# Splitting a unit's five blocks 4 + 1 instead of 3 + 2 over two transposing banks of an attention block

## The chip, the core and the metric

The kernel runs on one core of a Trainium2 chip. The metric is the device time of one execution in microseconds (us). Of the core's engines five matter here: TensorE (PE in the profile, its weight loads PEld), VectorE (DVE), ScalarE (ACT), GpSimd (POOL), and SyncE (SP), which issues the transfers. PSUM is the memory that TensorE writes to; it has banks of 512 fp32 columns.

## What is computed

One transformer block on 4096 tokens of 256 channels. A condition vector gives shifts, scales and gates; the first half is causal attention with 16 heads of 16 channels, whose softmax weights are multiplied by a decay of the distance; the second half a linear layer.

```python
mod = (_silu(L0_c) @ L0_wmod).reshape(L0_c.shape[0], 6, 1, -1)
...
h = _layernorm(x, axis=-1) * (1 + ca) + sa
x = x + ga * _L0_attn_ref(h, L0_attn_W_attn, L0_attn_W_proj)
h = _layernorm(x, axis=-1) * (1 + cb) + sb
x = x + gb * _L0_ffn_ref(h, ...)

# in _L0_attn_ref, for each head
att = jnp.einsum('bhqd,bhkd->bhqk', q, k) * (1.0 / math.sqrt(hd))
att = jnp.where(causal, att, -jnp.inf)
att = jax.nn.softmax(att, axis=-1)
att = att * decay_weight_matrix(T)
y = jnp.einsum('bhqk,bhkd->bhqd', att, v)
return y @ W_proj
```

The decay is zero from a distance of 512 on. So the softmax's sums need all keys, but the product with the values needs only the newest five blocks of 128 keys of each tile of 128 queries (`WIN = 5`; fewer for the first four tiles).

## The kernel before

A first stage forms queries, keys and values for all tokens and writes them out. Then `attention_fast` runs, of which all that follows speaks. (A slower form, `attention_full`, stands behind it in the program, for inputs on which the fast form's sums overflow.)

**Tiles and steps.** The 32 tiles of queries are taken in 16 pairs (`NPAIR`), a far tile (16 + p) and a near one (15 - p), so that all pairs have the same number of keys. A step s is one head of one pair: 256 steps (`NSTEP`). A unit is one head of one tile, so a step has a far and a near unit. `blocks(i)` is the number of a tile's blocks that meet the decay: five, but four for tile 3 and three to one for tiles 2 to 0, which are the near tiles of pairs 12 to 15.

**Scores and exponentials.** `split` cuts a tile's keys into chunks of up to 1024 columns; a step has five chunks in all (`PER`), in the order of `order(p)`: first far, second far, first near, and two more. TensorE's `fill(s, pos)` writes a chunk's scores into one of three slots of `fast_s_ps` and first waits until the exponential of three chunks before has read the slot; the newest chunk gets the causal mask by one more matmul (line 856). VectorE's `maximum` takes the row maximum of a unit's first chunk into `fast_negmax` (line 1082). ScalarE's `exponential` (line 1029) needs it: a unit's first chunk goes to `fast_probs`, of which there is one per side, and all others go back into their slot, since only their sums count. Before it writes `fast_probs`, it waits until the unit of the step before has been transposed out of it.

**Transposes and decay.** Two banks of PSUM (`fast_t_ps`, its second half `tail_ps`) take the transposed blocks of a unit. `turn` transposes the first `HEAD = 3` blocks into the first bank (line 871) and VectorE's `decay` multiplies them by the decay into `fast_probsT` (line 1091). `turn_tail` transposes the rest into the second bank (line 887), `decay_tail` takes them out (line 1101). Each bank has its own counters (`turn_full`, `turn_free`; `tail_full`, `tail_free`), and the lists `turn_no` and `tail_no` number the jobs that go through each bank, in one order: a job waits until the one before has left.

**Values.** Four heads (`HG`) of one tile are a group. `values(side, k, part)` forms the product of their decayed weights with the values (line 902) into the last 128 columns of the second bank, in two parts, which lie apart in TensorE's order; it waits until the tail jobs ahead of the group have left that bank. `group_to_sb` copies the result out (line 1107). A value matmul shows as two instructions in the profile. Behind the four heads' steps, far groups come in steps with s % 4 = 0, near groups in steps with s % 4 = 2 (`group_after`). Below, a step that has a group is called a group step.

**Other jobs.** What is left of a pair's work is done within the next pair's steps, by the tables `HEAD_JOBS` (through the first bank: steps 1, 3 and 13 of a pair) and `TAIL_JOBS` (through the second: the turning of y in step 5, the projections in 7 and 9, a transpose in 11, the linear layer in 13 and 15).

**The order.** Each engine's order is written out by hand. In TensorE's order the near unit's transposes come one step late, behind the next step's first scores; the far unit's stand between the fourth and the fifth chunk:

```python
fill(s, 0)
if s > 0:
    turn(NEAR, s - 1)
    turn_tail(NEAR, s - 1)
fill(s, 1)
fill(s, 2)
if group_after(s):
    values(*group_after(s), 0)
fill(s, 3)
...
turn(FAR, s)
if group_after(s):
    values(*group_after(s), 1)
    fill(s, 4)
    turn_tail(FAR, s)
```

In a step with a job of the second bank, the job stands in place of the second part of the values. VectorE's order in a step is: far maximum, near decay and tail decay of the step before, near maximum, the job of the first bank, far decay, the copy of the group or the job of the second bank, far tail decay.

Of the kernel before, what the change touches and what calls it, by code (L numbers as in the profile page):

```python
# [5 lines left out]
def bass_adaln_block_kernel(nc, x, w_attn, w_proj, ffn_wT, ffn_b, lora_downT, lora_upT, down_aux, up_auxT,  # L6
# [61 lines left out]
    def blocks(i):  # L68
        return min(WIN, i + 1)
# [125 lines left out]
    with ctx:  # L195
# [431 lines left out]
        def attention_fast():  # L627
# [16 lines left out]
            def tile_of(p, side):  # L644
                return NPAIR + p if side == FAR else NPAIR - 1 - p

            def turned(side, s):
                return TBASE[side] + s % TSLOTS[side]
# [19 lines left out]
            def step_of(s):  # L668
                return s // NH, s % NH


            HEAD = 3

            turn_no, tail_no = {}, {}

# [6 lines left out]
            def has_tail(side, s):  # L682
                return blocks(tile_of(s // NH, side)) > HEAD

# [72 lines left out]
            with s2:  # L757
# [80 lines left out]
                def _(pe):  # L838
# [21 lines left out]
                    def turn(side, s):  # L860
# [7 lines left out]
                        nb = blocks(i)  # L868
                        for b in range(min(HEAD, nb)):
                            lo = P * (b1 - b0 - nb + b)  # L870
# [3 lines left out]
                    def turn_tail(side, s):  # L874
# [9 lines left out]
                        nb = blocks(i)  # L884
                        for b in range(HEAD, nb):
                            lo = P * (b1 - b0 - nb + b)
                            last = nc.tensor.transpose(tail_ps[:, P * (b - HEAD):P * (b - HEAD + 1)],  # L887
                                                       probs[:, side, lo:lo + P], ident[:])
                        last.then_inc(tail_full, 1)

                    def values(side, k, part):

                        pe.wait_ge(tail_free, tail_no["group", side, k])
                        p, h = step_of(HG * k)
                        i = tile_of(p, side)
                        nb = blocks(i)
                        if h == 0 and part == 0:
                            pe.wait_ge(vals_loaded[p % 2], vals_count[p])
                        half = (nb + 1) // 2
                        for b in range(half) if part == 0 else range(half, nb):  # L900
                            for j in range(HG):
                                last = nc.tensor.matmul(g_ps[TC * j:TC * j + HD, :],  # L902
                                                        vals[:, side, (i + 1 - nb + b) % VT, HD * (h + j):HD * (h + j + 1)],
                                                        probsT[:, turned(side, HG * k + j), b, :],
                                                        start=(b == 0), stop=(b == nb - 1))
                                if b == nb - 1 and j == HG - 1:
                                    last.then_inc(tail_full, 1)
# [58 lines left out]
                    for s in range(NSTEP):  # L966
                        p, h = step_of(s)
                        if s % QH == 0:
                            u = s // QH
                            pe.wait_ge(q_loaded[u % 2], 16 * 2 * len(PAIRS) * (u // 2 + 1))  # L970
# [9 lines that stand above are left out]
                        if job_after(s, HEAD_JOBS):  # L980
                            head_job(*job_after(s, HEAD_JOBS))
# [5 lines that stand above are left out]
                        elif job_after(s, TAIL_JOBS):  # L987
                            tail_job(*job_after(s, TAIL_JOBS))
                            fill(s, 4)
                            turn_tail(FAR, s)  # L990
                        else:
                            turn_tail(FAR, s)
                            fill(s, 4)
# [3 lines left out]
                    for side in (FAR, NEAR):  # L997
                        for part in range(2):
                            values(side, NSTEP // HG - 1, part)
# [70 lines left out]
                def _(dve):  # L1070
# [15 lines left out]
                    def decay(side, s):  # L1086
                        dve.wait_ge(turn_full, turn_no["unit", side, s] + 1)
                        p, h = step_of(s)
                        nb = blocks(tile_of(p, side))
                        n = min(HEAD, nb)  # L1090
                        nc.vector.tensor_tensor(probsT[:, turned(side, s), 0:n, :],  # L1091
# [3 lines left out]
                    def decay_tail(side, s):  # L1095
                        if not has_tail(side, s):
# [3 lines left out]
                        nb = blocks(tile_of(p, side))  # L1100
                        nc.vector.tensor_tensor(probsT[:, turned(side, s), HEAD:nb, :],  # L1101
                                                tail_ps[:, 0:P * (nb - HEAD)].rearrange("p (b q) -> p b q", q=P),
# [510 lines left out]
        def rest_full():  # L1613
# [21 lines left out]
            with s3:  # L1635
# [164 lines left out]
                def _(dve):  # L1800
# [47 lines left out]
                    pipeline(dve, body)  # L1848

        attention_fast()  # L1850
        again = nc.values_load(redo[0:1, 0:1], min_val=0, max_val=1)
        with nc.If(again > 0):
# [43 lines left out]
```

## Time and profile before

| what | us |
|---|---|
| median of 3 runs | 1506.9 (1505.77 to 1508.43) |
| the profiled execution | 1504.86 |
| its span, first to last instruction | 1502.3 |
| ScalarE busy | 1298.8 (86%) |
| TensorE busy, matmuls | 1263.3 (84%) |
| VectorE busy | 1000.9 (67%) |
| GpSimd busy | 204.2 (14%) |

The first 165 us or so form queries, keys and values; the loop of 256 steps then runs to about 1470 us, and the last pair's jobs end the span. Busy shares are means over these stages. To find what a change in the loop's order is worth, read a stretch out of the loop's middle: first the busy times in it, then who waits for whom, then the timeline of single steps, in which the end of one row can be held against the start of the next on another engine. Rows of matmuls overlap, and their ends are modelled; the start of a row says more than its length. A timeline row takes together instructions of one shape that follow each other, and a row's place is where its first one starts.

### The profile page before, as it was taken

To read this page: it belongs to the slowest core of one execution; us is meant where nothing else is said; L and a number is where in the kernel's file an instruction comes from. 1 tells how busy PE (TensorE), PEld (TensorE's weight loads), DVE (VectorE), ACT (ScalarE), POOL (GpSimd) and SP (SyncE) were. 2 spreads that over 40 slices of the span, in tenths; PEclk is the share of its full clock that TensorE was granted. 3 is DMA by queue.
4 is the path that set the end of the run, shared out by engine and by line. 5 is a ranking of instruction groups with operands and counts; after the bars stand their busy time and mean duration, and the time that the engine had idled before them with its cause. 6 is when DMAs were issued, how large, how long until landed. Compare 5 with 4: busy or idle time off the path is not lost.

```text
span 1502.3 us, 28806 instructions
## 1 busy us (share of the span) xinstructions
PE 1263.3 (84%) x11067; PEld 745.0 (50%) x11067; DVE 1000.9 (67%) x2058; ACT 1298.8 (86%) x2628; POOL 204.2 (14%) x429
## 2 busy tenths in 40 slices
PE   7994588989888898888888998988898888887774
PEld 5552345555555555555555555555555444444432
DVE  4843477777777777777777777777776766665452
ACT  2552699999999999999999999999999999999880
POOL 0331000110202020202011020202020201111022
PEclk9996799999999999999999999999999999999996
DMA  4797300000000000000000000000000000000000
GB/s 154 240 302 263 106 12 12 19 26 19 15 19 14 23 19 26 19 25 19 26 19 23 17 14 22 16 26 19 26 16 25 15 26 15 26 15 19 8 4 13
DMA packets 94448, 64.63 MB, mean 43 GB/s; under 512 B 59595, under 2 KB 89570, under 8 KB 94306
## 3 DMA queue, kind: packets, MB, share of 16 engines
q1 hardware_dynamic: 94306, 62.75, 14.1%
q8 instruction: 87, 1.43, 0.4%
q14 instruction: 55, 0.45, 0.1%
HBM read 41.74 MB, written 20.97 MB: 42 GB/s over the span
## 4 chain that ended last, share of the span: by engine, by line
PE 39%; DVE 27%; ACT 13%; issue 9%; POOL 1%; SPq 0%; DMA 0%; ACTq 0%; DVEq 0%
PE fast_s_ps L853 13%; DVE fast_negmax L1082 12%; PE fast_t_ps L902 10%; ACT fast_s_ps L1029 8%; DVE fast_probsT L1101 7%; PE fast_t_ps L871 5%; PE fast_t_ps L887 5%; ACT fast_probs L1029 5%; PE fast_t_ps L931 4%; DVE fast_probsT L1091 4%; DVE fast_y_sb L1120 1%; DVE fast_xb L1134 1%; DVE fast_xb L1157 1%; PE fast_t_ps L913 1%; DVE fast_tT L1127 1%
## 5 line engine op out<-in xcount | busy, mean ns | idle before, releaser
L1029 ACT ACTIVATE fast_s_ps<-fast_s_ps,fast_negmax 128x1024 f32<-128x1024 f32 (+4 forms) x768 | 786.6, 1026 | 12.4 <-PE fast_s_ps L853 11.7
L853 PE MATMUL fast_s_ps<-k_stack,fast_q_stack 96*128 96x512 bf16 (+3 forms) x2448 | 643.2, 354 | 118.1 <-ACT fast_probs L1029 83.5
L1029 ACT ACTIVATE fast_probs<-fast_s_ps,fast_negmax 128x640 f32<-128x640 f32 (+7 forms) x512 | 431.7, 843 | 62.1 <-DVE fast_negmax L1082 57.8
L1082 DVE TENSOR_REDUCE fast_negmax<-fast_s_ps 128x1 f32<-128x640 f32 (+4 forms) x512 | 397.9, 777 | 35.9 <-PE fast_s_ps L856 20.2
L1091 DVE TENSOR_TENSOR fast_probsT<-fast_t_ps,fast_dec_c 128x384 f32<-128x384 f32 (+2 forms) x512 | 276.6, 540 | 202.8 <-PE fast_t_ps L871 202.7
L853 PEld LDWEIGHTS fast_s_ps<-k_stack,fast_q_stack 96*128 96x128 bf16 x2448 | 202.4, 98 | 321.4 <-ACT fast_probs L1029 137.2
L871 PE MATMUL fast_t_ps<-ident,fast_probs 128*128 128x128 f32 x1488 | 252.0, 276 | 29.4 <-DVE fast_y_sb L1120 20.8
L1101 DVE TENSOR_TENSOR fast_probsT<-fast_t_ps,fast_dec_c 128x256 f32<-128x256 f32 x464 | 192.4, 415 | 114.7 <-PE fast_t_ps L887 114.7
L871 PEld LDWEIGHTS fast_t_ps<-ident,fast_probs 128*128 128x128 f32 x1488 | 171.8, 142 | 84.1 <-DVE fast_y_sb L1120 28.1
L887 PE MATMUL fast_t_ps<-ident,fast_probs 128*128 128x128 f32 x912 | 195.9, 295 | 19.9 <-DVE fast_tT L1127 6.4
L902 PE MATMUL fast_t_ps<-fast_probsT,fast_vals 128*16 128x128 f32 x4800 | 179.8, 275 | 23.4 <-DVE fast_probsT L1101 21.9
L1029 ACT ACTIVATION_READ_ACCUMULATOR fast_s_ps<-fast_s_ps,fast_negmax 128x1 f32 x768 | 163.6, 213 | 0.0
L1048 POOL TENSOR_SCALAR fast_var_e<-fast_mv 128x1 f32<-128x1 f32 x32 | 7.3, 228 | 1129.5 <-DVE fast_mv L1142 1129.4
L887 PEld LDWEIGHTS fast_t_ps<-ident,fast_probs 128*128 128x128 f32 x912 | 97.2, 141 | 118.7 <-DVE fast_yT_sb L1107 47.9
L902 PEld LDWEIGHTS fast_t_ps<-fast_probsT,fast_vals 128*16 128x16 f32 x4800 | 109.1, 96 | 71.3 <-DVE fast_probsT L1101 45.8
L856 PE MATMUL fast_s_ps<-causal,ident_b 128*128 128x128 bf16 x512 | 113.3, 221 | 0.0
L1029 ACT ACTIVATION_READ_ACCUMULATOR fast_probs<-fast_s_ps,fast_negmax 128x1 f32 x512 | 104.2, 203 | 0.0
L856 PEld LDWEIGHTS fast_s_ps<-causal,ident_b 128*128 128x128 bf16 x512 | 49.8, 97 | 54.9 <-issue 1.4
L392 ACT CAST part<-kq 128x2048 bf16<-128x2048 f32 x8 | 15.2, 1898 | 39.7 <-issue 20.2
L404 POOL TENSOR_TENSOR part<-kq,part 128x2048 bf16<-128x2048 f32 (+1 forms) x8 | 32.0, 4000 | 103.2 <-ACT part L392 103.2
L1054 POOL TENSOR_SCALAR fast_rstd<-fast_root_t,fast_three_halves,fast_rstd 128x1 f32<-128x1 f32 x128 | 44.0, 344 | 12.9
L1053 POOL TENSOR_SCALAR fast_root_t<-fast_rstd,fast_var_h 128x1 f32<-128x1 f32 x128 | 44.0, 344 | 12.9
(110 smaller groups left out, 723.7 us busy)
## 6 DMA issues: line engine op xcount, KB each, us to landing
parts_d<-part SPq DMA_DIRECT2D x24, 512.0 KB, 4.3
k_stack<-parts_d SPq DMA_DIRECT2D x96, 128.0 KB, 3.0
fast_q_stack<-parts_d SPq DMA_DIRECT2D x384, 32.0 KB, 2.1
fast_vals<-v_d SPq DMA_DIRECT2D x36, 128.0 KB, 2.5
xs<-x_dram SPq DMA_DIRECT2D x8, 512.0 KB, 6.6
v_d<-w SPq DMA_DIRECT2D x8, 512.0 KB, 5.7
fast_xb<-x_dram SPq DMA_DIRECT2D x32, 128.0 KB, 2.1
out_dram<-fast_xb SPq DMA_DIRECT2D x32, 128.0 KB, 2.0
```

Source lines behind the costliest of these rows:

```text
L853: last = nc.tensor.matmul(s_ps[:, n % SLOTS, o:o + w], q, k_stack[:, h, P * b0 + o:P * b0 + o + w], start=True, stop=not diag)
L856: last = nc.tensor.matmul(s_ps[:, n % SLOTS, o + w - P:o + w], ident_b[:], causal[:], start=False, stop=True)
L871: last = nc.tensor.transpose(t_ps[:, P * b:P * (b + 1)], probs[:, side, lo:lo + P], ident[:])
L887: last = nc.tensor.transpose(tail_ps[:, P * (b - HEAD):P * (b - HEAD + 1)], probs[:, side, lo:lo + P], ident[:])
L902: last = nc.tensor.matmul(g_ps[TC * j:TC * j + HD, :], vals[:, side, (i + 1 - nb + b) % VT, HD * (h + j):HD * (h + j + 1)], probsT[:, turn ...
L931: last = nc.tensor.matmul(tail_ps[:, 0:C], tT[:, side, cc, :], weights[:, cc, :], start=(cc == 0), stop=(cc == CH - 1))
L1029: nc.scalar.activation(dst, src, ACT.Exp, bias=negmax[:, p % 2, side, h:h + 1], scale=-1.0, accum_out=sums[:, p % 2, side, h, c:c + 1]).th ...
L1053: chained(nc.gpsimd.tensor_scalar(w, y, y, half, ALU.mult, ALU.mult))
L1054: chained(nc.gpsimd.tensor_scalar(y, w, three_halves[:, 0:1], y, ALU.add, ALU.mult))
L1082: nc.vector.tensor_reduce(out=negmax[:, p % 2, side, h:h + 1], in_=s_ps[:, n % SLOTS, max(0, cols - P * WIN):cols], axis=AX_X, op=ALU.min) ...
L1091: nc.vector.tensor_tensor(probsT[:, turned(side, s), 0:n, :], t_ps[:, 0:P * n].rearrange("p (b q) -> p b q", q=P), dec_c[:, WIN - nb:WIN - ...
L1101: nc.vector.tensor_tensor(probsT[:, turned(side, s), HEAD:nb, :], tail_ps[:, 0:P * (nb - HEAD)].rearrange("p (b q) -> p b q", q=P), dec_c[ ...
```

## The change

The first bank takes four blocks of a unit and the second one, in place of three and two. The first part of a group's values goes over as many blocks as the first bank takes, in place of the larger half (for five blocks four in place of three).

```diff
-            HEAD = 3
+            HEAD = 4
...
-                        half = (nb + 1) // 2
+                        half = min(HEAD, nb)
```

`HEAD` is read in `has_tail`, `turn`, `turn_tail`, `decay` and `decay_tail`. A unit of four blocks no longer has a tail: this is the near unit of pair 12. For tiles of four blocks or fewer the second part of the values becomes empty, and the first takes all of them (four blocks 4 + 0 in place of 2 + 2, three 3 + 0 in place of 2 + 1, two 2 + 0 in place of 1 + 1).

On TensorE, in a group step of a pair with five blocks, from the first part of the values (line 902) to the mask of the next step's first scores (line 856), before:

```order
L902 MATMUL fast_t_ps<-fast_probsT,fast_vals 16x128 x12
L853 MATMUL fast_s_ps<-k_stack,fast_q_stack 128x512 x2
L871 MATMUL fast_t_ps<-ident,fast_probs 128x128 x3
L902 MATMUL fast_t_ps<-fast_probsT,fast_vals 16x128 x8
L853 MATMUL fast_s_ps<-k_stack,fast_q_stack 128x512
L853 MATMUL fast_s_ps<-k_stack,fast_q_stack 128x384
L887 MATMUL fast_t_ps<-ident,fast_probs 128x128 x2
L853 MATMUL fast_s_ps<-k_stack,fast_q_stack 128x512
L853 MATMUL fast_s_ps<-k_stack,fast_q_stack 128x128
L856 MATMUL fast_s_ps<-causal,ident_b 128x128
```

The same stretch of TensorE's order now:

```order
L902 MATMUL fast_t_ps<-fast_probsT,fast_vals 16x128 x16
L853 MATMUL fast_s_ps<-k_stack,fast_q_stack 128x512 x2
L871 MATMUL fast_t_ps<-ident,fast_probs 128x128 x4
L902 MATMUL fast_t_ps<-fast_probsT,fast_vals 16x128 x4
L853 MATMUL fast_s_ps<-k_stack,fast_q_stack 128x512
L853 MATMUL fast_s_ps<-k_stack,fast_q_stack 128x384
L887 MATMUL fast_t_ps<-ident,fast_probs 128x128
L853 MATMUL fast_s_ps<-k_stack,fast_q_stack 128x512
L853 MATMUL fast_s_ps<-k_stack,fast_q_stack 128x128
L856 MATMUL fast_s_ps<-causal,ident_b 128x128
```

Four value matmuls moved from behind the far unit's first transposes to ahead of them, and one transpose from ahead of the next step's scores to the place ahead of the second part of the values.

On VectorE, from the far maximum (line 1082) of a group step to the next step's far maximum, before (`fast_dec_c` holds the decay):

```order
L1082 TENSOR_REDUCE fast_negmax<-fast_s_ps 128x1
L1091 TENSOR_TENSOR fast_probsT<-fast_t_ps,fast_dec_c 128x384
L1101 TENSOR_TENSOR fast_probsT<-fast_t_ps,fast_dec_c 128x256
L1082 TENSOR_REDUCE fast_negmax<-fast_s_ps 128x1
L1091 TENSOR_TENSOR fast_probsT<-fast_t_ps,fast_dec_c 128x384
L1107 COPY fast_yT_sb<-fast_t_ps 128x128
L1101 TENSOR_TENSOR fast_probsT<-fast_t_ps,fast_dec_c 128x256
L1082 TENSOR_REDUCE fast_negmax<-fast_s_ps 128x1
```

The same stretch of VectorE's order now:

```order
L1082 TENSOR_REDUCE fast_negmax<-fast_s_ps 128x1
L1091 TENSOR_TENSOR fast_probsT<-fast_t_ps,fast_dec_c 128x512
L1101 TENSOR_TENSOR fast_probsT<-fast_t_ps,fast_dec_c 128x128
L1082 TENSOR_REDUCE fast_negmax<-fast_s_ps 128x1
L1091 TENSOR_TENSOR fast_probsT<-fast_t_ps,fast_dec_c 128x512
L1107 COPY fast_yT_sb<-fast_t_ps 128x128
L1101 TENSOR_TENSOR fast_probsT<-fast_t_ps,fast_dec_c 128x128
L1082 TENSOR_REDUCE fast_negmax<-fast_s_ps 128x1
```

The order is the same; 128 columns moved from the decay behind the group's copy to the decay ahead of it.

## Rows read from the trace of the kernel before

**Rows 1.** Busy times by stretch: window, length, then PE, PEld, DVE, ACT, POOL; PEclk, DMA

```profile
600.00:700.00 100.00, 87.16 (x864) 53.59 (x854) 73.59 (x148) 94.95 (x197) 12.41 (x32) 1.00 0.09 23
```

**Rows 2.** ScalarE's waits, whole span: us in total, times, longest

```profile
ACT fast_probs L1029 <- DVE fast_negmax L1082: 57.8, 141, 10.6
```

**Rows 3.** Timeline of ScalarE (start, length): pairs 0 and 11, after a group step

```profile
189.01 0.80 ACT L1029 ACTIVATE fast_probs<-fast_s_ps,fast_negmax 128x640 f32<-128x640 f32 x1 [0.27 <-DVE fast_negmax L1082]
...
1136.31 0.79 ACT L1029 ACTIVATE fast_probs<-fast_s_ps,fast_negmax 128x640 f32<-128x640 f32 x1 [0.33 <-DVE fast_negmax L1082]
```

**Rows 4.** Timeline of a group step in pair 5, from far maximum to the next step

```profile
608.03 0.82 DVE L1082 TENSOR_REDUCE fast_negmax<-fast_s_ps 128x1 f32<-128x640 f32 x1
...
608.77 0.55 DVE L1091 TENSOR_TENSOR fast_probsT<-fast_t_ps,fast_dec_c 128x384 f32<-128x384 f32 x1
...
609.23 0.41 DVE L1101 TENSOR_TENSOR fast_probsT<-fast_t_ps,fast_dec_c 128x256 f32<-128x256 f32 x1
...
609.70 0.85 PE L902 MATMUL fast_t_ps<-fast_probsT,fast_vals 128*16 128x128 f32 x24 [0.38 <-DVE fast_probsT L1101]
...
610.48 0.50 PE L853 MATMUL fast_s_ps<-k_stack,fast_q_stack 96*128 96x512 bf16 x2
...
610.82 0.49 PE L871 MATMUL fast_t_ps<-ident,fast_probs 128*128 128x128 f32 x3
...
611.24 0.63 PE L902 MATMUL fast_t_ps<-fast_probsT,fast_vals 128*16 128x128 f32 x16
611.35 0.56 DVE L1091 TENSOR_TENSOR fast_probsT<-fast_t_ps,fast_dec_c 128x384 f32<-128x384 f32 x1 [0.64 <-PE fast_t_ps L871]
...
611.64 0.88 ACT L1029 ACTIVATE fast_s_ps<-fast_s_ps,fast_negmax 128x768 f32<-128x768 f32 x1
...
611.80 0.60 PE L853 MATMUL fast_s_ps<-k_stack,fast_q_stack 96*128 96x512 bf16 x2
611.94 0.29 DVE L1107 COPY fast_yT_sb<-fast_t_ps 128x128 f32<-128x128 f32 x1
...
612.28 0.44 PE L887 MATMUL fast_t_ps<-ident,fast_probs 128*128 128x128 f32 x2
...
612.51 1.10 ACT L1029 ACTIVATE fast_s_ps<-fast_s_ps,fast_negmax 128x1024 f32<-128x1024 f32 x1
612.56 0.49 PE L853 MATMUL fast_s_ps<-k_stack,fast_q_stack 96*128 96x512 bf16 x2
...
612.88 0.22 PE L856 MATMUL fast_s_ps<-causal,ident_b 128*128 128x128 bf16 x1
...
613.14 0.82 DVE L1082 TENSOR_REDUCE fast_negmax<-fast_s_ps 128x1 f32<-128x640 f32 x1
...
614.00 0.90 ACT L1029 ACTIVATE fast_probs<-fast_s_ps,fast_negmax 128x768 f32<-128x768 f32 x1 [0.27 <-DVE fast_negmax L1082]
```

**Rows 5.** Timeline of a step with a projection, the one before that

```profile
605.29 0.49 PE L871 MATMUL fast_t_ps<-ident,fast_probs 128*128 128x128 f32 x3
...
605.62 1.03 PE L931 MATMUL fast_t_ps<-wp_g,fast_tT 128*128 128x256 f32 x4
...
605.82 0.56 DVE L1091 TENSOR_TENSOR fast_probsT<-fast_t_ps,fast_dec_c 128x384 f32<-128x384 f32 x1 [0.42 <-PE fast_t_ps L871]
...
606.69 0.42 DVE L1134 TENSOR_TENSOR fast_xb<-fast_xb,fast_t_ps 128x256 f32<-128x256 f32 x1 [0.31 <-PE fast_t_ps L931]
```

**Rows 6.** Timeline of a step that turns y, in pair 10: VectorE

```profile
1005.76 0.56 DVE L1091 TENSOR_TENSOR fast_probsT<-fast_t_ps,fast_dec_c 128x384 f32<-128x384 f32 x1 [0.42 <-PE fast_t_ps L871]
...
1006.24 0.68 DVE L1127 COPY fast_tT<-fast_t_ps 128x512 f32<-128x512 f32 x1
```

**Rows 7.** Timeline, TensorE: first value part and next scores in pairs 12 and 14

```profile
1171.98 0.63 PE L902 MATMUL fast_t_ps<-fast_probsT,fast_vals 128*16 128x128 f32 x16
...
1172.55 0.61 PE L853 MATMUL fast_s_ps<-k_stack,fast_q_stack 96*128 96x512 bf16 x2
...
1341.98 0.60 PE L853 MATMUL fast_s_ps<-k_stack,fast_q_stack 96*128 96x512 bf16 x2 [0.37 <-ACT fast_probs L1029]
```

## The prediction, made before the changed kernel ran

> **What bounds the kernel now.** The stage table comes first. In a stretch out of the middle ScalarE is busy 94.95 of 100 us, TensorE's rows 87, VectorE 74, at full granted clock [rows 1]. So ScalarE sets the pace there, and a step of one head costs at least its five exponentials. The list of ScalarE's waits comes next: its longest wait by far is 57.8 us in 141 places, an exponential into `fast_probs` for the row maximum from VectorE [rows 2]. The two ends of a series show its place: the first of a step's five exponentials, in the step after one with value matmuls; it is there in the first pair of tiles and 950 us later [rows 3]. The reader is to see that the loop is not bound by ScalarE alone: once a step it stands still for a chain through VectorE and TensorE, so anything that lengthens this chain lengthens the kernel.
>
> The timeline shows the chain of such a group step [rows 4]. Maximum 608.03; decay of the head 608.77 and of the tail 609.23, ended 609.64; for that the first part of the values waits (0.38 us) and starts at 609.70; score matmuls 610.48; three transposes 610.82; second part 611.24; scores 611.80. VectorE can start the far decay only at 611.35 (it waited 0.64 us for the transposes), then copies the group out, 611.94 to 612.23; for that copy TensorE's tail transposes wait, since both lie in one bank (612.28); behind them stand the next step's first scores (612.56) with the mask (612.88); behind these the next maximum (613.14) and the exponential (614.00, 0.27 us idle before). TensorE has no gap in this chain that would take up more work. Steps come with a group in turn with steps that have another job at that place.
>
> **The change, part by part.** No engine gets more work in sum. The five transposes of a unit stay five. The two decays cost 0.55 and 0.41 us now [rows 4]; for 512 and 128 columns no decay is to be seen, but copies from the same banks are: 0.68 us at 512 columns [rows 6] and 0.29 us at 128 [rows 4]. 0.96 us stands against 0.97. Value matmuls stay 40 instructions a group. So only the place of the work counts, and I walk the chain of the group step.
>
> The start does not move: the first value part still waits for the near unit's tail decay, and head and tail together end where they did (0.96 against 0.97); the one more transpose ahead of them lies beside the maximum of 0.82 us.
> - First value part, four blocks in place of three, 32 instructions in place of 24. From its start to the next scores 24 take 0.78 us [rows 4], 16 take 0.57 [rows 7]: +0.21.
> - Fourth transpose in the far head: three take 0.33 us from start to the next work [rows 5]: +0.11.
> - Wider head decay, 0.68 in place of 0.55: +0.13.
> - The copy of the group. Two ops in a row on VectorE start 0.09 us before the first one's row ends (609.23 against 608.77 + 0.55). After its decay (to 611.91) the copy could thus have started at 611.82, but started at 611.94, with the end of the second value part (611.87). That part gets 0.21 shorter: it starts 0.32 later and ends 0.11 later, while the decay ends 0.45 later. So the copy is now late for the decay alone, and 0.12 of the 0.45 is lag it had already: -0.12.
> - One transpose less in the tail ahead of the next scores: two take 0.28 us in the rows, entry included; at the pitch above -0.11.
>
> Together 0.21 + 0.11 + 0.13 - 0.12 - 0.11 = +0.22 us at the next scores. The maximum starts 0.26 us after its mask matmul did, now as then; the tail decay ahead of it ends about 0.1 us sooner than that, so TensorE sets it. ScalarE was waiting already (0.27 us idle), so all of 0.22 goes into the time. Behind the longer value part the scores for the fourth exponential (611.64) come at 610.98 + 0.21, in time; those for the fifth end at 612.40 + 0.11, just as it starts (612.51); what that may cost lies in front of the wait that follows and is hidden by it.
>
> How many: 256 steps, 126 group steps in the loop (none in the first four steps, then every other one: 6 in the first pair, 8 in each later one). In pairs 0 to 11 every tile, near ones too (tiles 15 to 4), has five blocks, so the walk holds: 6 + 88 = 94 steps. 94 x 0.22 = 20.7 us.
>
> The other steps. Where the job is a matmul (project, linear), the fourth transpose puts the job 0.11 later, the tail's missing one gives 0.11 back, and the wider decay lies beside it: the job's reader starts at 606.69, 0.31 us after the decay (605.82 + 0.56) [rows 5]. Zero, as long as that 0.31 covers 0.13. Where the job is the turning of y, no such cover is there: the 512-wide copy starts at 1006.24 straight after the decay (1005.76 + 0.56) [rows 6], so 0.11 + 0.13 - 0.11 = +0.13, in 15 steps: 2.0 us. In steps with a head job five transposes stand in a row before and after: zero.
>
> Late pairs. In pair 12 the near tile has four blocks: its tail disappears (16 decays less), and the two value parts go from 16 + 16 instructions to 32 + 0. The first then costs 0.43 more, of which some 0.2 is won since it need not wait for a near tail decay: about +0.27 in each of three steps there, and as much once in pair 13; four far groups in pair 13 cost about 0.2 each; together 2.2 us, my estimate from the same pitches. From pair 14 on TensorE is idle 0.37 us before the scores that follow the first value part [rows 7], which covers the 0.21: nothing.
>
> **Sum.** 20.7 + 2.0 + 2.2 = 24.9 us. The profiled execution took 1504.86 us (span 1502.3), which gives 1529.8; it is 2 us under the median 1506.9, which gives 1531.8. I take 1531.
>
> **Bounds.** The copy's lag is the softest term. If it was no lag, the step costs 0.34, 94 x 0.34 + 6 = 38 us: 1544. If the missing tail transpose is worth 0.14 (half of 0.28) and the wider decay 0.10, the step costs 0.16, 15 + 3 = 18 us: 1523.
>
> **Rivals.**
> ScalarE hides it. If ScalarE alone sets the time, a shift on TensorE changes nothing: 1505 to 1508. For it: 95% busy. Against: the 0.27 us in front of every such step's exponential, which is no reserve but a wait already. The Trainium skill, "Perfetto Trace Analysis", section "Identifying the Most-Contended Engine", says to find the bottleneck by occupancy, which for ScalarE is a fair measure of how close it is to its roofline. By that rule the result would be this rival's; the waits here speak against it.
>
> Faster. The tail sits right in front of the next scores, and a tail of one transpose and 0.28 us brings scores and maximum forward by 0.11 in each step with a wait, some 150 of them, if the head's added transpose and value block find an idle TensorE: 94 x (0.11 + 0.12) or, more carefully, 150 x 0.11 = 16 us less: 1490. It decides by a gap of 0.32 us (0.21 + 0.11) before the scores that follow the first value part. In pair 14 there is one of 0.37; in the group step shown there is none, the scores start with the values' end.
>
> Larger. The late fifth scores and the copy without lag both add up: 0.22 + 0.12 + 0.11 = 0.45, 94 x 0.45 + 5 = 47 us: 1553. It needs the fifth exponential's delay to push the chain itself, and its slot is asked for only by the next step's third scores.
>
> **How the numbers follow.** Forecast with its bounds 0.75, ScalarE hides it 0.07, faster 0.06, larger 0.07, smaller than the lower bound but still slower 0.05. The range 1514 to 1546 takes in both bounds and most of that last case, and leaves out 0.2. Within 0.2% (3 us, about what a measurement of this kernel can tell) lies the first rival: same 0.07, faster 0.06, slower 0.87.
>
> **What would show it.** In the profile after: the idle time before the first exponential of a step that follows a group step rises from 0.27 to about 0.5 us, in all of pairs 0 to 11 and at the same places, and ScalarE's total for that wait by some 21 us; the decay of the head takes 0.68, that of the tail 0.28; the copy starts straight after the decay and no longer after the second value part; the tail transposes still wait for the copy; steps with project or linear keep their length. It is wrong if the step's first value part starts earlier than the near tail decay's end, if 32 value instructions take as long as 24 to the next work, or if the exponential's wait shrinks.

## The result and the profile after

The changed kernel takes 1536.4 us (median of 4 runs, 1531.6 to 1538.2) against 1506.3 before: ratio 1.0201, 95% interval 1.0179 to 1.0223. It is 30 us slower, in the range given and 5 us above the forecast of 1531. The profiled execution took 1537.74 us, its span is 1535.2.

The page's first part, of the changed kernel: engine, busy us, share of the span, instructions.

```profile
PE 1267.1 (83%) x11067; PEld 754.0 (49%) x11067; DVE 1001.1 (65%) x2042; ACT 1301.9 (85%) x2628; POOL 204.2 (13%) x429
```

No engine has much more to do: ScalarE is busy 1301.9 us for 1298.8, VectorE 1001.1 for 1000.9, TensorE 1267.1 for 1263.3. So most of the 33 us in the span are waits. ScalarE's list of waits says which (us in total, times, longest); this is the row that answers to [rows 2]:

```profile
ACT fast_probs L1029 <- DVE fast_negmax L1082: 81.6, 152, 10.7
```

57.8 us have become 81.6: 23.8 us more in the one wait that was named. One more wait of the loop has grown, by 4.5 us: the wait for scores of a later chunk. Most of that, 3.4 us, lies in the late pairs, which are taken up below. Its row before, then after:

```profile
ACT fast_s_ps L1029 <- PE fast_s_ps L853: 11.7, 22, 2.3
```

```profile
ACT fast_s_ps L1029 <- PE fast_s_ps L853: 16.2, 25, 2.2
```

The first exponential of the group step of [rows 4], in the kernel before:

```profile
608.89 0.90 ACT L1029 ACTIVATE fast_probs<-fast_s_ps,fast_negmax 128x768 f32<-128x768 f32 x1
```

The timeline of the changed kernel, the same group step of pair 5:

```profile
619.02 0.82 DVE L1082 TENSOR_REDUCE fast_negmax<-fast_s_ps 128x1 f32<-128x640 f32 x1
...
619.88 0.90 ACT L1029 ACTIVATE fast_probs<-fast_s_ps,fast_negmax 128x768 f32<-128x768 f32 x1
...
620.69 1.07 PE L902 MATMUL fast_t_ps<-fast_probsT,fast_vals 128*16 128x128 f32 x32 [0.39 <-DVE fast_probsT L1101]
...
621.69 0.50 PE L853 MATMUL fast_s_ps<-k_stack,fast_q_stack 96*128 96x512 bf16 x2
...
622.03 0.60 PE L871 MATMUL fast_t_ps<-ident,fast_probs 128*128 128x128 f32 x4
...
622.56 0.41 PE L902 MATMUL fast_t_ps<-fast_probsT,fast_vals 128*16 128x128 f32 x8
...
622.63 0.88 ACT L1029 ACTIVATE fast_s_ps<-fast_s_ps,fast_negmax 128x768 f32<-128x768 f32 x1
622.67 0.69 DVE L1091 TENSOR_TENSOR fast_probsT<-fast_t_ps,fast_dec_c 128x512 f32<-128x512 f32 x1 [0.96 <-PE fast_t_ps L871]
622.90 0.60 PE L853 MATMUL fast_s_ps<-k_stack,fast_q_stack 96*128 96x512 bf16 x2
623.27 0.28 DVE L1107 COPY fast_yT_sb<-fast_t_ps 128x128 f32<-128x128 f32 x1
...
623.55 1.09 ACT L1029 ACTIVATE fast_s_ps<-fast_s_ps,fast_negmax 128x1024 f32<-128x1024 f32 x1
...
623.61 0.33 PE L887 MATMUL fast_t_ps<-ident,fast_probs 128*128 128x128 f32 x1
623.78 0.49 PE L853 MATMUL fast_s_ps<-k_stack,fast_q_stack 96*128 96x512 bf16 x2
623.98 0.29 DVE L1101 TENSOR_TENSOR fast_probsT<-fast_t_ps,fast_dec_c 128x128 f32<-128x128 f32 x1 [0.42 <-PE fast_t_ps L887]
624.11 0.22 PE L856 MATMUL fast_s_ps<-causal,ident_b 128*128 128x128 bf16 x1
...
624.36 0.82 DVE L1082 TENSOR_REDUCE fast_negmax<-fast_s_ps 128x1 f32<-128x640 f32 x1
...
625.22 0.90 ACT L1029 ACTIVATE fast_probs<-fast_s_ps,fast_negmax 128x768 f32<-128x768 f32 x1 [0.47 <-DVE fast_negmax L1082]
```

Hold these rows against the earlier ones by differences. From the first value part to the next scores 1.00 us, for 0.78. From the far transposes to the second part 0.53, for 0.42. The decay 0.69, for 0.56. The copy starts at 623.27, which is 0.09 before the decay's row ends (622.67 + 0.69); the second value part has ended by 622.97, so the copy no longer waits for it. From the copy's start to the next maximum 1.09, for 1.20, since one transpose left. The step, from exponential to exponential, takes 5.34 us (619.88 to 625.22) for 5.11 (608.89 to 614.00), and the idle time in front of the last row is 0.47 for 0.27.

The same reckoning for all 256 steps (start of each step's first exponential, by the two traces): in the 94 group steps of pairs 0 to 11 the median step is 0.23 us longer, 21.9 us in sum; the 11 steps that turn y there 0.13 to 0.14 each, 1.5 us; the other steps there 1.0 us. Pairs 12 to 15 take 7.7 us more (0.6, 2.0, 2.4, 2.6). What is left of the 33 us, 0.9, lies ahead of the loop and behind it.

### The profile page after: what moved, and what is told of

Read it like the earlier page. It is cut to its first block, busy times and chain, and to the rows that moved or that the text cites. A ratio compares the mean times of both kernels' runs of the same rounds, so it can differ in the third digit from the quotient of the medians.

```text
span 1535.2 us, 28802 instructions
## 1 busy us (share of the span) xinstructions
PE 1267.1 (83%) x11067; PEld 754.0 (49%) x11067; DVE 1001.1 (65%) x2042; ACT 1301.9 (85%) x2628; POOL 204.2 (13%) x429
## 4 chain that ended last, share of the span: by engine, by line
PE 39%; DVE 30%; ACT 10%; issue 9%; POOL 1%; SPq 0%; DMA 0%; ACTq 0%; DVEq 0%
PE fast_s_ps L853 14%; DVE fast_negmax L1082 12%; DVE fast_probsT L1091 10%; PE fast_t_ps L871 8%; PE fast_t_ps L902 8%; ACT fast_s_ps L1029 6%; PE fast_t_ps L887 4%; ACT fast_probs L1029 4%; PE fast_t_ps L931 4%; DVE fast_yT_sb L1107 2%; DVE fast_probsT L1101 1%; PE fast_s_ps L856 1%; DVE fast_y_sb L1120 1%; DVE fast_xb L1134 1%; DVE fast_xb L1157 1%
## 5 line engine op out<-in xcount | busy, mean ns | idle before, releaser
L1091 DVE TENSOR_TENSOR fast_probsT<-fast_t_ps,fast_dec_c 128x512 f32<-128x512 f32 (+3 forms) x512 | 338.6, 661 | 258.3 <-PE fast_t_ps L871 258.2
L1029 ACT ACTIVATE fast_probs<-fast_s_ps,fast_negmax 128x640 f32<-128x640 f32 (+7 forms) x512 | 431.2, 842 | 86.7 <-DVE fast_negmax L1082 81.6
L853 PEld LDWEIGHTS fast_s_ps<-k_stack,fast_q_stack 96*128 96x128 bf16 x2448 | 214.6, 102 | 318.2 <-ACT fast_probs L1029 141.1
L871 PE MATMUL fast_t_ps<-ident,fast_probs 128*128 128x128 f32 x1952 | 305.5, 277 | 30.0 <-DVE fast_y_sb L1120 20.7
L871 PEld LDWEIGHTS fast_t_ps<-ident,fast_probs 128*128 128x128 f32 x1952 | 223.7, 142 | 88.2 <-DVE fast_y_sb L1120 28.0
L1101 DVE TENSOR_TENSOR fast_probsT<-fast_t_ps,fast_dec_c 128x128 f32<-128x128 f32 x448 | 128.3, 286 | 91.4 <-PE fast_t_ps L887 91.4
L887 PE MATMUL fast_t_ps<-ident,fast_probs 128*128 128x128 f32 x448 | 135.0, 301 | 47.7 <-DVE fast_yT_sb L1107 19.3
L887 PEld LDWEIGHTS fast_t_ps<-ident,fast_probs 128*128 128x128 f32 x448 | 62.9, 140 | 142.7 <-DVE fast_yT_sb L1107 78.6
```

Source lines behind the costliest of these rows:

```text
L853: last = nc.tensor.matmul(s_ps[:, n % SLOTS, o:o + w], q, k_stack[:, h, P * b0 + o:P * b0 + o + w], start=True, stop=not diag)
L871: last = nc.tensor.transpose(t_ps[:, P * b:P * (b + 1)], probs[:, side, lo:lo + P], ident[:])
L1029: nc.scalar.activation(dst, src, ACT.Exp, bias=negmax[:, p % 2, side, h:h + 1], scale=-1.0, accum_out=sums[:, p % 2, side, h, c:c + 1]).th ...
```

## The experiments

All ratios are against the kernel before on the same chip, with 95% intervals. The step that is quoted from a trace is always the same, the group step of pair 5 above. The theory is a chain: values ahead of the far transposes, far transposes, far decay, the group's copy, tail transposes, next scores, maximum, exponential. Its first rival says that each displaced length costs by itself; its second that the split over the banks does it.

**The banks alone.**

```diff
-            TSLOTS = {FAR: HG, NEAR: HG + 2}
-            TBASE = {FAR: 0, NEAR: HG}
+            TSLOTS = {FAR: HG + 1, NEAR: HG + 2}
+            TBASE = {FAR: 0, NEAR: HG + 1}
...
-            HEAD = 3
+            HEAD = 4
```

> Only the banks go 4 + 1; the value parts stay three and two blocks. (The far side of fast_probsT gets a fifth slot, since the wider head would otherwise overwrite a block that the second value part still reads; this has no time of its own.) Theory, the chain through the group's copy: in a group step the fourth transpose puts the second value part's end 0.11 us later and the far decay's end 0.24 later; the copy, which lagged 0.12 behind the decay before, starts 0.12 later; one tail transpose less gives 0.11 back; so +0.01 per group step, +0.13 in the 15 steps that turn y, and up to 3 us in the late pairs: +2 to +6 us, ratio 1.001 to 1.004. Rival, each displaced length counts by itself: transposes and decay cost 0.13 in each of 94 steps, 12 us, and 2 to 5 more: ratio about 1.010. Rival, the banks are the whole cause: 1.020.

Measured 1.0019 (1.0004 to 1.0035), as the chain has it. Timeline of ScalarE, first exponentials of that step and the next:

```profile
608.85 0.90 ACT L1029 ACTIVATE fast_probs<-fast_s_ps,fast_negmax 128x768 f32<-128x768 f32 x1
...
613.97 0.90 ACT L1029 ACTIVATE fast_probs<-fast_s_ps,fast_negmax 128x768 f32<-128x768 f32 x1 [0.25 <-DVE fast_negmax L1082]
```

5.12 us for 5.11: +0.01; the steps that turn y take 0.13 to 0.14 more. Both rivals that give the banks a price of their own (1.010 and 1.020) lie outside the interval.

**The value parts alone.**

```diff
-                        half = (nb + 1) // 2
+                        half = min(4, nb)
```

> Only the value parts go 4 + 1; the banks stay 3 + 2. Theory, the chain through the group's copy: the far transposes start 0.21 us later and the far decay ends 0.21 later, the second value part ends where it did; of the 0.21 the copy's lag of 0.12 takes its share; +0.09 per group step, 94 x 0.09 = 8.5 us, and 1 to 3 in the late pairs: +9 to +12 us, ratio 1.006 to 1.008. Together with the banks alone this is less than the change's 30 us, because the lag is used up once. Rival, the longer first value part counts by itself: 94 x 0.21 = 20 us, ratio 1.013 to 1.015. Rival, the banks are the cause: 1.000.

Measured 1.0061 (1.0034 to 1.0089), at the lower end of the forecast; both rivals lie outside the interval. The same two rows:

```profile
611.67 0.90 ACT L1029 ACTIVATE fast_probs<-fast_s_ps,fast_negmax 128x768 f32<-128x768 f32 x1
...
616.88 0.90 ACT L1029 ACTIVATE fast_probs<-fast_s_ps,fast_negmax 128x768 f32<-128x768 f32 x1 [0.37 <-DVE fast_negmax L1082]
```

5.21 us: +0.10 (median of the 94 steps 0.09, 9.1 us in sum). So the two halves of the change cost 0.01 and 0.09 alone and 0.23 together. Lengths that add up by themselves can't do this. A stretch of slack that is spent once can. The banks alone end the decay 0.24 later and shorten the tail by 0.11, the value parts alone end the decay 0.21 later, both together 0.45 later. The copy's lag of 0.12 behind the decay comes off once in each case: 0.24 - 0.12 - 0.11 = 0.01, 0.21 - 0.12 = 0.09, 0.45 - 0.12 - 0.11 = 0.22.

**The copy ahead of the decay.** In the changed kernel, VectorE's order:

```diff
-                        decay(FAR, s)
                         if group_after(s):
                             group_to_sb(*group_after(s))
+                        decay(FAR, s)
```

> The changed kernel, with VectorE's copy of the group ahead of the far decay in its order, not behind it. Theory: the copy then starts with the end of the second value part (622.97 in the changed kernel's timeline) and not after the decay (623.27), the tail transposes and the next scores come 0.26 us earlier per group step, which is 0.04 earlier than in the kernel before: 94 x 0.26 = 24 us of the 30 come back, what is left is the steps that turn y (2 us) and the late pairs (4 to 7): ratio against the kernel before 1.002 to 1.005. Rival, the value part and the transposes cost what they do because TensorE has to issue them earlier, whatever VectorE does behind: stays at 1.018 to 1.021.

Measured 1.0006 (0.9994 to 1.0019), just below the forecast: the 30 us are gone, with two instructions of VectorE exchanged in 126 steps and TensorE's order as in the changed kernel. The timeline there:

```profile
620.50 0.90 ACT L1029 ACTIVATE fast_probs<-fast_s_ps,fast_negmax 128x768 f32<-128x768 f32 x1
...
623.18 0.41 PE L902 MATMUL fast_t_ps<-fast_probsT,fast_vals 128*16 128x128 f32 x8
...
623.66 0.29 DVE L1107 COPY fast_yT_sb<-fast_t_ps 128x128 f32<-128x128 f32 x1 [1.34 <-PE fast_t_ps L902]
623.87 0.68 DVE L1091 TENSOR_TENSOR fast_probsT<-fast_t_ps,fast_dec_c 128x512 f32<-128x512 f32 x1
624.00 0.33 PE L887 MATMUL fast_t_ps<-ident,fast_probs 128*128 128x128 f32 x1
...
624.47 0.28 DVE L1101 TENSOR_TENSOR fast_probsT<-fast_t_ps,fast_dec_c 128x128 f32<-128x128 f32 x1
...
625.61 0.90 ACT L1029 ACTIVATE fast_probs<-fast_s_ps,fast_negmax 128x768 f32<-128x768 f32 x1 [0.24 <-DVE fast_negmax L1082]
```

The copy now starts with the end of the second value part, and TensorE's tail transpose (624.00) right behind it, while VectorE still works on the far decay. This settles the place: not TensorE's longer pieces but the copy behind them, in VectorE's queue, is what the next scores wait for. The step takes as long as in the kernel before (5.11 us), not 0.04 less as expected. The copy starts 3.16 us behind the step's first exponential where the changed kernel has 3.39, and this 0.23 is all that the step wins: the copy still starts 0.07 behind the end of the second value part's row (623.18 + 0.41), as it did in the kernel before (611.94 against 611.87), and the expectation had let it start at that end.

By the traces the loop wins 21 us back in pairs 0 to 11, of the 24 forecast. The late pairs, for which 4 to 7 us were to be left, take 3.4 us less than in the kernel before: 1.2 of it in steps in which the granted clock falls in one of the two traces, 2.2 in the others. That is why the ratio lies below the forecast.

**All values first, copy first.** If the copy is the link, a group whose values all stand ahead of the far transposes should lose the link altogether. From the kernel before, with banks 3 + 2 and the order of VectorE as just shown:

```diff
-                        half = (nb + 1) // 2
+                        half = nb
```

> The kernel before (banks 3 + 2), with all five blocks of a group's values in the first part, none in the second, and VectorE's copy of the group ahead of the far decay. Theory: the first part grows by 0.42 us, the second part's 0.56 disappears, and the copy is over before the far transposes are; so the tail transposes wait for the fifth chunk's scores alone and come 0.28 us earlier per group step: 94 x 0.28 = 26 us less in pairs 0 to 11, little in the late ones: ratio 0.980 to 0.986. Rival, more values ahead of the far transposes always cost (0.21 per block): 94 x 0.42 = 39 us more, ratio 1.02 or above. Rival, ScalarE is the bound and nothing is to be had: 1.000.

Measured 0.9763 (0.9736 to 0.9789), 1467.8 us: faster than both kernels, and below the forecast. The timeline:

```profile
594.10 0.90 ACT L1029 ACTIVATE fast_probs<-fast_s_ps,fast_negmax 128x768 f32<-128x768 f32 x1
...
594.92 1.29 PE L902 MATMUL fast_t_ps<-fast_probsT,fast_vals 128*16 128x128 f32 x40 [0.38 <-DVE fast_probsT L1101]
...
596.27 0.29 DVE L1107 COPY fast_yT_sb<-fast_t_ps 128x128 f32<-128x128 f32 x1 [0.34 <-PE fast_t_ps L902]
596.47 0.49 PE L871 MATMUL fast_t_ps<-ident,fast_probs 128*128 128x128 f32 x3
...
597.24 0.38 PE L887 MATMUL fast_t_ps<-ident,fast_probs 128*128 128x128 f32 x2
...
598.90 0.90 ACT L1029 ACTIVATE fast_probs<-fast_s_ps,fast_negmax 128x768 f32<-128x768 f32 x1
```

The first value part is 40 instructions long, the copy done at 596.56 and the tail transposes far behind it. The step takes 4.80 us, 0.31 less than before, and no wait stands before the last row. In pair 10 the group steps are 0.43 shorter. ScalarE's total for this wait:

```profile
ACT fast_probs L1029 <- DVE fast_negmax L1082: 29.4, 42, 10.6
```

Of 141 waits 42 are left. In the group steps of pairs 0 to 11 the gain is 35.8 us, 10 more than forecast. The forecast walked a step of pair 5, whose fifth chunk has 1024 columns, and nothing but this chunk's scores now stands between the far transposes and the tail. The gain goes by that chunk's width: step 6 of a pair gains 0.32 us where it has 1024 columns (pairs 4 to 7), 0.37 at 896 (3 and 11), 0.43 at 768 (2 and 10) and 0.46 at 640 and 512 (1, 9 and 8). That fewer scores let the tail come sooner is the likely reason; no run tests it alone.

**The same with the copy left behind the decay.** The diff above alone, VectorE's order as in the kernel before.

> The kernel before with all of a group's values in the first part, and the copy left behind the far decay. Theory: far transposes and decay come 0.42 us later, the copy that lagged 0.12 behind the decay comes 0.30 later, and with it the tail transposes and the next scores: 94 x 0.30 = 28 us more in pairs 0 to 11 and some in the late ones: ratio 1.018 to 1.022. Rival, what made values_first fast is that the values stand in one piece, not the place of the copy: ratio 0.98 or below here too.

Measured 1.025 (1.0219 to 1.0281), above the forecast's 1.018 to 1.022. In the group steps of pairs 0 to 11 it is +0.31 for the 0.30 forecast, 29.4 us in sum; where the rest lies is open. The same two rows:

```profile
622.23 0.90 ACT L1029 ACTIVATE fast_probs<-fast_s_ps,fast_negmax 128x768 f32<-128x768 f32 x1
...
627.66 0.90 ACT L1029 ACTIVATE fast_probs<-fast_s_ps,fast_negmax 128x768 f32<-128x768 f32 x1 [0.60 <-DVE fast_negmax L1082]
```

By the ratios the same move of TensorE's work makes the slowest of all kernels here with the copy behind the decay, and the fastest with the copy ahead of it. The rival, that the values in one piece made the gain, falls.

**Values first, copy first, banks 4 + 1.** The diff of the banks (`HEAD = 4`) on top of the fastest kernel.

> Values first, copy ahead of the far decay (as in values_first), and in addition the banks 4 + 1. Theory: with the copy out of the way the five far transposes stand nearly in a row before the next scores, as in a step with a head job, so 4 + 1 against 3 + 2 costs nothing in the group step; the steps that turn y cost 0.13 each: 0 to 4 us more than values_first, ratio against the kernel before 0.976 to 0.980. Rival, a head of four is what costs: 94 x 0.13 = 12 us more than values_first, ratio 0.984.

Measured 0.9799 (0.9775 to 0.9823), the upper end of the theory's range; the rival's 0.984 lies outside the interval. In the group steps of pairs 0 to 11 it gains 33.7 us where the fastest gains 35.8, and the steps that turn y cost their 1.5; 4 + 1 has no gain in this order either.

**Early and late pairs apart.** The change in pairs 0 to 11 only, and in pairs 12 to 15 only (`HEAD` and the value parts chosen by the pair):

```diff
-            HEAD = 3
+            def head_of(p):
+                return 4 if p < 12 else 3
...
-                        half = (nb + 1) // 2
+                        half = min(4, nb) if p < 12 else (nb + 1) // 2
```

> Banks 4 + 1 and values 4 + 1 in pairs 0 to 11 only, pairs 12 to 15 as before. Theory: what the change costs in these pairs is 0.22 us in each of 94 group steps and 0.13 in each of 11 steps that turn y, with what else the changed kernel's trace shows there 24 us; the late pairs keep their time: +22 to +26 us, ratio 1.015 to 1.018. Rival, the change's extra in the late pairs (7.7 us by the two traces) is noise of single executions and not of the change: then this kernel is as slow as the change, 1.020.

Measured 1.0183 (1.0161 to 1.0206). The interval holds the theory's upper end and the rival's 1.020, so the ratio doesn't decide between them. By the trace pairs 0 to 11 take 24.3 us more, pairs 12 to 15 0.6 us less.

> Banks 4 + 1 and values 4 + 1 in pairs 12 to 15 only, pairs 0 to 11 as before. By the traces of before and of the change these pairs take 7.7 us more, of which about 4.3 lie in three steps in which the granted clock falls to its lower level. Theory A, the falls come with the change, since it leaves TensorE idle longer in these pairs: +5 to +9 us, ratio 1.003 to 1.006, with three or four falls in pairs 13 to 15. Theory B, the falls are chance: +2 to +4 us, ratio 1.001 to 1.003, with one or two falls as before.

Measured 1.0059 (1.0038 to 1.0081). By the trace pairs 12 to 15 take 5.2 us more, with four falls of the granted clock in pairs 13 to 15. The two parts add up to 1.024, more than the change's 1.020. A little of that is counted twice: the last two groups of pair 11, formed in the first steps of pair 12, are changed in both kernels. With intervals of 0.002 each the ratios tell no more than that the late pairs have a share of some 3 to 9 us.

## Why the prediction was right, and where it was short

- *What bounds.* ScalarE stands still once a step for a chain through VectorE and TensorE. Shown: its busy time stayed, its wait for the maximum grew by 23.8 us, and a kernel that shortens the chain took 36 us off.
- *ScalarE hides it.* ScalarE is the busiest engine, and the change doesn't touch its work; the rival that rests on this expected no change. The measured 2% speak against it for this kernel, and the fastest kernel shows both sides: once the chain is short enough, a step costs what ScalarE needs.
- *The group step.* +0.22 forecast, 0.23 measured (median of 94), and term by term: value block 0.21 against 0.22, transpose 0.11 and 0.11, decay 0.13 and 0.13, the tail's missing transpose 0.11 and 0.11. The copy's lag, the softest term, was real: the copy starts straight behind the decay now, and the two halves of the change alone cost 0.01 and 0.09.
- *Faster and larger.* Faster needed a gap on TensorE in front of the next scores; they come 0.22 later, and ScalarE's wait grew. Larger needed the late scores of the fifth chunk and a copy without lag to add up: the fifth exponential does start a little late (0.92 us behind the fourth for 0.87), but ahead of the wait that follows, which hides it, as the prediction's walk has it.
- *The steps that turn y.* +0.13 forecast, 0.13 to 0.14 measured, in the changed kernel and with the banks alone, and none with the value parts alone.
- *Project and linear steps.* Zero forecast; steps 7, 9, 13 and 15 of pairs 1 to 11 change by 0.01 at most.
- *Steps with a head job.* Zero forecast, and not quite right: steps 1 and 3 of pairs 1, 2, 8, 9 and 10 take 0.03 to 0.12 more each, 0.7 us in sum. The transpose in step 11, which the prediction doesn't speak of, adds 0.10 and 0.14 in pairs 6 and 7. Pairs 1, 2, 8, 9 and 10 are those whose fifth chunk has 768 columns or fewer; what the delay goes through there was not followed.
- *The late pairs.* 2.2 us (and 0.5 for turning y) forecast, 7.7 in the trace. The terms written out for the 2.2 (four of 0.27 and four of 0.2) add up to 1.9. In the 55 of the 63 steps in which TensorE's granted clock falls in neither trace, the change costs 2.7 us; the other 5.0 us lie in eight steps in which it falls in one or both. Of the clock the prediction said nothing. The steps without a fall give the same in the kernel with the change in the late pairs alone: 2.8 us in 57 steps.
- *Luck.* That these 2.7 us meet the forecast is partly luck, since the parts came out otherwise. The near groups of pair 12 cost 0.11, 0.12, -0.06 and 0.26 for 0.27 each, the far groups of pair 13 cost 0.23, 0.06, 0.10 and 0.01 for 0.2 each. "From pair 14 on nothing" was wrong: the near group steps there take 0.12 to 0.14 more, the far ones 0.00 to 0.09, about 1 us. TensorE's idle 0.37 us does cover the longer value part, but not the fourth transpose and the wider decay behind it: in pair 14 the near group steps take 0.00 more with the value parts alone, and 0.12 to 0.13 with the banks alone.

The granted clock of TensorE in the changed kernel, by stretches in pairs 13 to 15 (window, length, busy us of PE, PEld, DVE, ACT and POOL, then the granted clock as a share of 2.4 GHz):

```profile
1300.00:1312.00 12.00, 9.60 (x88) 4.94 (x87) 8.03 (x16) 11.80 (x25) 5.38 (x13) 1.00 0.01 2
1312.00:1316.00 4.00, 3.48 (x13) 2.31 (x12) 1.29 (x3) 2.53 (x6) 0.00 (x0) 0.68 0.01 2
...
1364.00:1368.00 4.00, 3.53 (x11) 2.49 (x12) 0.88 (x3) 3.06 (x8) 0.00 (x0) 0.58 0.00 0
...
1418.00:1422.00 4.00, 3.41 (x15) 2.02 (x14) 1.31 (x3) 2.70 (x7) 0.00 (x0) 0.66 0.44 136
1428.00:1436.00 8.00, 6.40 (x23) 3.49 (x23) 2.90 (x8) 5.21 (x11) 0.00 (x0) 0.59 0.00 0
```

The first stretch is at the full 2.4 GHz; each of the other four is at the lower level, 1.2 GHz, for part of its time. What that does to a step is seen in the timeline of the first fall:

```profile
1311.83 0.60 PE L853 MATMUL fast_s_ps<-k_stack,fast_q_stack 96*128 96x512 bf16 x2 [0.79 <-ACT fast_probs L1029]
...
1313.17 0.92 PE L871 MATMUL fast_t_ps<-ident,fast_probs 128*128 128x128 f32 x4 [0.52 <-DVE fast_tT L1151]
...
1313.88 1.91 PE L931 MATMUL fast_t_ps<-wf_g,fast_tT 128*128 128x256 f32 x4
...
1316.68 1.09 ACT L1029 ACTIVATE fast_s_ps<-fast_s_ps,fast_negmax 128x1024 f32<-128x1024 f32 x1 [2.16 <-PE fast_s_ps L853]
```

TensorE had waited 0.79 us for ScalarE and 0.52 for VectorE; then four transposes take 0.92 us in place of 0.60, a linear layer 1.91 in place of the 1.03 that these four matmuls take in a projection [rows 5], and ScalarE waits 2.16 us. This step is 1.4 us longer than before. There are five such falls within pairs 13 to 15 of the changed kernel and two in the kernel before; four of the five are in the stretches shown.

Whether the change brings these falls is not settled. For it: four of them with the change in the late pairs alone, two with the change in the early pairs alone. Against a firm statement: it is one trace each, and in the other kernels' late pairs there are one to four. With the change in the early pairs alone, the late pairs run the code of the kernel before, and yet the falls lie in other steps: in step 1 of pairs 14 and 15, for steps 3 and 13 of pair 15. Within the changed kernel's own runs the time goes with the mean granted clock: spans of 1535.2 and 1536.5 us at 0.966, 1533.3 at 0.968, 1529.8 at 0.972.

## What to carry to other kernels

Where two jobs share a bank, ask which instruction frees it, and what stands ahead of that instruction in its engine's queue: here a copy of 0.28 us stood behind a decay that it has nothing to do with, and every delay of the decay beyond the copy's lag of 0.12 went on to the next scores. Before a piece of work is moved to an earlier place, look whether its result is taken out where it now ends; moved together with its reader it won 2.4%, moved alone it lost 2.5%. A lag that covers a delay is spent once: two changes that are free or cheap one by one (0.01 and 0.09) cost 0.23 together.

## What the runs showed of the hardware beyond what was expected

- Value matmuls with 16 rows of output each add 0.21 to 0.22 us per 8 instructions, on top of a share per piece: to the next scores 16 took 0.57, 24 took 0.78, 32 took 1.00 and 40 took 1.22 us (594.92 to 596.14 in the fastest kernel).
- VectorE's multiplication out of PSUM takes 0.28 to 0.29 us for 128 columns and 0.68 to 0.69 for 512, the same as its copies [rows 4, 6].
- TensorE's clock falls within the late pairs to 1.2 GHz. In the changed kernel, the kernel before and the one with the change in the early pairs alone, a fall there costs 1.2 to 2.2 us in the one or two steps that it touches.
